# Local attention in one kernel: units of four heads by 128 keys, stacked blocks of 64 queries, and a rotary sum moved to GpSimd

## The reference

```
h = shift_token(x); q, k, v = split(h @ wqkv)
q, k = rotary_xpos(l2norm(q) * qs, l2norm(k) * ksc)
sim = (8 q) k^T over the keys of a query's own block of 64 and of the block before
      masked where key > query or key < query - 64
x = x + softmax(sim) v @ wo
x = x + feed_forward(layer_norm(shift_token(x)))
```

## Time and profile before

| what | value |
|---|---|
| time before, median of 3 runs | 2269.81 us (2269.67 to 2273.56) |
| the profiled execution, its own time | 2267.61 us |
| its span in the profile | 2265.8 us |
| mean granted TensorE clock over the span | 0.938 |
| busy over the span: PE, DVE, ACT, POOL | 1887.1, 1730.5, 1326.7, 840.5 us |

### The profile page before, as it was taken

One profiled execution on the slowest core, in us unless ns is written; L12 is line 12 of the kernel. 1 busy time (PEld: TensorE's weight loads), 2 busy tenths in 40 slices (PEclk: granted clock), 3 DMA queues, 4 the chain that ended last, 5 costly groups with the idle time before them and its releaser, 6 DMA issues. The chain is left out here.

```text
span 2265.8 us, 38842 instructions
## 1 busy us (share of the span) xinstructions
PE 1887.1 (83%) x12576; PEld 1040.6 (46%) x12576; DVE 1730.5 (76%) x4306; ACT 1326.7 (59%) x2865; POOL 840.5 (37%) x703
## 2 busy tenths in 40 slices
PE   6888888875898988769717579999999999999985
PEld 2333333332444444434315346666656566666543
DVE  6999999994677777412166679999986899999875
ACT  5777777731444444324252368888873688888731
POOL 5777777751022222224421433333321333333211
PEclk8999999995999999879958889999999999999997
DMA  5333333203011111023171400000001000000011
GB/s 152 116 100 113 109 115 117 89 29 99 23 36 43 39 37 43 23 82 109 45 210 51 132 24 6 6 1 1 2 4 26 1 6 6 1 1 1 4 35 29
DMA packets 102297, 117.06 MB, mean 52 GB/s; under 512 B 27780, under 2 KB 78255, under 8 KB 101104
## 3 DMA queue, kind: packets, MB, share of 16 engines
q1 hardware_dynamic: 98000, 106.51, 16.1%
q0 software_dynamic: 4096, 8.06, 1.1%
HBM read 71.44 MB, written 38.11 MB: 48 GB/s over the span
## 5 line engine op out<-in xcount | busy, mean ns | idle before, releaser
L392 POOL TENSOR_TENSOR m_bu<-m_dtu,m_brow 128x1024 f32<-128x1024 f32 x128 | 300.4, 2360 | 58.8 <-DVE m_hs L807 57.0
L807 DVE TENSOR_TENSOR_SCAN m_hs<-m_ps_da,m_bu 128x1024 f32<-128x1024 f32 x128 | 291.9, 2281 | 3.6 <-POOL m_bu L392 2.5
L1355 ACT ACTIVATE a_pt<-a_ps_s 128x1024 f32<-128x1024 f32 x128 | 131.1, 1025 | 227.5 <-PE a_ps_s L1133 227.5
L2851 ACT ACTIVATE l_pe<-l_ps_s,l_nbias,l_qs 128x192 f32<-128x192 f32 (+1 forms) x512 | 244.8, 487 | 32.3 <-DVE l_nbias L3007 32.3
L513 PE MATMUL m_ps_y_ps<-m_prod,m_ident 128*128 128x512 f32 x512 | 248.4, 608 | 0.0
L1472 DVE TENSOR_REDUCE a_mpad<-a_ps_s 128x4 f32<-128x1024 f32 x128 | 156.8, 1225 | 93.7 <-PE a_ps_s L1125 92.7
L1125 PE MATMUL a_ps_s<-a_heads 32*128 32x256 f32 x1024 | 187.9, 447 | 44.3 <-DVE a_mpad L1472 28.5
L659 ACT ACTIVATE m_ps_da<-m_dt,m_a_neg 128x510 f32<-128x510 f32 x256 | 166.0, 681 | 72.2 <-DVE m_hs L807 71.9
L1133 PE MATMUL a_ps_s<-a_qm,a_heads 32*128 32x256 f32 x1024 | 184.7, 437 | 1.8 <-ACT a_pt L1355 1.4
L2623 PE MATMUL l_ps_s<-l_kT,l_qT 128*128 128x384 f32 (+1 forms) x512 | 179.9, 433 | 0.0
L2861 ACT COPY l_pT<-l_ps_t 128x256 f32<-128x256 f32 (+1 forms) x256 | 122.9, 480 | 72.5 <-PE l_ps_t L2633 45.8
(11 more groups left out here) (336 smaller groups left out, 4454.6 us busy)
## 6 DMA issues: line engine op xcount, KB each, us to landing
m_brow<-state_rows SPq DMA_DIRECT2D x64, 512.0 KB, 4.3
slots<-m_void SPq DMA_DIRECT2D x16, 516.0 KB, 5.4
e_xs<-slots SPq DMA_DIRECT2D x16, 258.0 KB, 2.7
ys<-m_void SPq DMA_DIRECT2D x8, 512.0 KB, 5.4
qk<-a_qk SPq DMA_DIRECT2D x16, 256.0 KB, 2.0
a_heads<-qk SPq DMA_DIRECT2D x64, 64.0 KB
ew_w<-in_w SPq DMA_DIRECT2D x2, 2048.0 KB, 11.6
e_yy<-ys SPq DMA_DIRECT2D x16, 256.0 KB, 5.4
```

Source lines behind the costliest of these rows:

```text
L392: nc.gpsimd.tensor_tensor(bu[s % 4][:, :, :], dtu[p][:, :, :], b2, ALU.mult).then_inc(bu_rd, 1)
L807: dve.tensor_tensor_scan(hs[s % 4][:, :, :].rearrange("p h t -> p (h t)"), da[s % 2][:, :, :, :].rearrange("p h q t -> p (h q t)"), bu[s % ...
L2851: nc.scalar.activation(pe_[u % 2][:, h, 0:nk], s_ps[u % 2][:, h * 192:h * 192 + nk], ACT.Exp, bias=nbias[:, u % 2, h:h + 1], scale=qs[b % ...
```

## The change

It rewrites the attention of both local layers and leaves the feed-forward as it is.

- A unit is now four heads by 128 keys (`HU = 4`, `NU = 2` units a chunk, `U = 4` units a sequence). `maxima`, `exps`, `divide`, `transpose_p` and `p_copy` work on 4 x 128 columns in both chunks. `divide` is one product with a broadcast operand in place of one scaling per head.
- In chunk 1 each block of 64 queries has its own window of 128 keys, and the two blocks are stacked on partitions 0 to 63 and 64 to 127 of the same bank: four matmuls with 64 stationary columns in place of one with 128. `weigh` in chunk 1 takes 64 columns at a time, eight matmuls a unit, all with fresh accumulation.
- The first block's values lie across the two chunks. `bring_near` on SP copies them into a buffer `near` in the right order of partitions, by two DMAs from SBUF to SBUF a sequence, and PE waits for them ahead of chunk 1's first `weigh`. SP issues it ahead of `gather` in its queue.
- The queries' `rotary_sum` goes from DVE to POOL (the keys' stays on DVE).
- `hT` is doubled, `v` has three buffers in place of four, the waits follow.
- All three `attend` functions are written out anew, with another order, shown below for PE and DVE.

```
     def scores(n, b, u):
...
+        at_least(pe, l.ex_rd, HU * (i - 1))
+        bank = s_ps[u % 2][:, :].rearrange("p (h k) -> p h k", h=HU)
+        pe.matmul(bank, identb[:, :], mask[:, c, :, :], start=True, stop=False, ...)
+        for k in range(2):
+            j = 2 * d + k
+            if c == 0:
+                last = pe.matmul(bank[:, 2*k:2*k+2, :], qT[p][:, j, 0:P], kT[p][:, :, j, 0:P], ...)
+            else:
+                for r in range(2):
+                    q0 = P + r * HD
+                    last = pe.matmul(bank[r*HD:(r+1)*HD, 2*k:2*k+2, :], qT[p][:, j, q0:q0+HD],
+                                     kT[p][:, :, j, q0-HD:q0+HD], ...)
+        last.then_inc(l.s_mm, 1)
...
     def weigh(n, b, u):
+        else:      # chunk 1: for k, r, h
+            vals = near[(NB * n + b) % 2][:, :] if r == 0 else v[z][:, 1, :]
+            last = pe.matmul(dst, vals[:, cols], pT[u % 2][:, 2*k+h, r*HD:(r+1)*HD], start=True, ...)
...
     def divide(n, b, u):
+        dve.wait_ge(l.ex_rd, HU * (i + 1))
+        dve.reciprocal(ri[:, :], rs[:, u % 2, :]).then_inc(l.ri_s, 1)
+        dve.tensor_tensor(pn[u % 2][:, :, :], pe_[u % 2][:, :, :],
+                          ri[:, :].unsqueeze(2).to_broadcast([P, HU, P]), ALU.mult).then_inc(l.pn_rd, 1)
...
     def bring_near(n, b):                                        # SP
+        sp.wait_ge(l.v_sb, NCH * (b + 1))
+        sp.dma_start(near[k % 2][0:HD, :], v[z][HD:P, 0, :]).then_inc(near_in, 16)
+        sp.dma_start(near[k % 2][HD:P, :], v[z][0:HD, 1, :]).then_inc(near_in, 16)
...
     def rotary_sum(l, b, c):                                     # POOL, queries
+        pool.wait_ge(l.rot_rd[Q], i + 1)
+        nc.gpsimd.tensor_tensor(c1[Q][:, :, :], c1[Q][:, :, :], c2[Q][:, :, :], ALU.add)...
```

More of the change, by code:

```diff
@@ new lines, in attend @@
+                    scores(n, b, 0)
+                    if not first:
+                        transpose_p(n, b - 1, U - 1)
+                    if last < 2:
+                        project(n, b + 1, 0, Q)
+                    if not first:
+                        weigh(n, b - 1, U - 2)
+                        if last < 2:
+                            pe.wait_ge(l.v_sb, NCH * (b + 1))
+                        else:
+                            pe.wait_ge(l.res_rd, NCH * (b - 1))
+                        output(n, b - 1, 0)
@@ new lines, in attend @@
+                    scores(n, b, 1)
+                    transpose_p(n, b, 0)
+                    turn_k(n, b, 1)
+                    if not first:
+                        weigh(n, b - 1, U - 1)
+                    if last < 2:
+                        turn_q(n, b + 1, 0)
+                        if not first:
+                            pe.wait_ge(l.res_rd, NCH * (b - 1) + 1)
+                        project_v(n, b + 1, 0)
+                        project(n, b + 1, 0, K)
+                    scores(n, b, 2)
@@ new lines, in attend @@
+                    if not first:
+                        square_sums(n, b, 1, K)
+                        divide(n, b - 1, U - 1)
+                    if last < 2:
+                        rotary(n, b + 1, 0, Q)
+                    if not first:
+                        residual(n, b - 1, 0)
+                    scale_k(n, b, 1)
+                    maxima(n, b, 1)
+                    if last < 2:
+                        square_sums(n, b + 1, 0, Q)
+                    divide(n, b, 0)
+                    if last < 2:
+                        rotary(n, b + 1, 0, K)
+                        rotary_sum(n, b + 1, 0, K)
@@ new lines, in attend @@
+                    maxima(n, b, 2)
+                    if last < 2:
+                        square_sums(n, b + 1, 0, K)
+                    divide(n, b, 1)
+                    if last < 2:
+                        rotary(n, b + 1, 1, Q)
+                    if not first:
+                        residual(n, b - 1, 1)
+                    if last < 2:
+                        scale_k(n, b + 1, 0)
+                    else:
+                        norm_stats(n, 0)
+                    maxima(n, b, 3)
@@ L3050, in norm_stats @@
+                    if last < 2:
+                        square_sums(n, b + 1, 1, Q)
+                    divide(n, b, 2)
+                    if last < 2:
+                        rotary(n, b + 1, 1, K)
+                        rotary_sum(n, b + 1, 1, K)
                 def norm_stats(n, g):
```

332 lines of the change are left out of this document (157 added, 175 removed).

## The result

| | kernel before | kernel after |
|---|---|---|
| median of 4 runs | 2269.74 us (2269.61 to 2273.56) | 2647.24 us (2643.44 to 2666.53) |
| ratio, 95% interval | | 1.1672 [1.1627, 1.1717] |
| span of the profiled execution | 2265.8 us | 2648.0 us |
| mean granted clock over the span | 0.938 | 0.887 |

The change makes the kernel 377 us slower, by the medians. The forecast was 2622 us, range 2485 to 2745. Of the 382 us between the two spans, 366 lie in the two attention stages, from the first scores to the first feed-forward matmul: 374.2 us became 561.8, and 375.1 became 553.1. The rest lies at the layers' starts, between the first `transpose_r` and the first stage (4.7 us) and between the two stages (6.4 us), and 5.7 us in stretches that the change doesn't touch.

The account below looks back on a forecast made before the run. PE was taken as the bound, busy 22.86 of 23.56 us a sequence. Work 20.2 plus waits 11.3 gave 31.5, with clock falls 35.0; (35.0 - 23.56) x 31 = 355 us on 2267.6 gave 2622 us, range 2485 to 2745.

Parts of the forecast that it names:

- the sign: In the profile, `transpose_p` would wait for DVE's probabilities 2.5 to 3.3 us in every unit, 128 times.
- The round trip: PE idles from scores until DVE's maxima, `square_sums` and `divide` end: 2.51 us a unit, all waits 11.3 a sequence.
- the extra in the keys' two steps: In two steps DVE does the keys' rotary and sum before the maxima, lengthening PE's wait by 0.77 and 0.47 us.
- PE's own work: Transposes, scores and weighing in the new units: PE's work falls from 22.86 to 20.2 us a sequence.
- the 2.3 end: Chunk 1 scores per unit if changing tiling mode drains the array without overlap: 2.3 us, 1.8 a sequence more.
- The 0.3 in the sum for entering and leaving the form: Chunk 1 scores: about 0.3 us a unit for switching into and out of half-width matmuls, within the 1.40 taken.
- Period at full clock: One attention sequence without clock falls: 20.2 work plus 11.3 waits, 31.5 us against 23.56.
- About two falls in four waits: PE's clock drops after some attention waits, each fall costing 1.63 us; the sequence is taken as 35.0 us.
- The clock stays up: Rival: attention waits never lower PE's clock; 2513 us, or 2495 with half-width forms at their low ends; chance 0.18.
- The second rival: Half-width matmuls run one after the other and the clock falls after every wait: 2784 us, milder 2700 to 2750; chance 0.12.
- What the rest costs: nothing.: In attention, DVE's, ACT's and POOL's changed work and the DMAs of `near` stay covered; POOL's added sum is 1.2 us.
- a rival with 0.05: Attention waits are hidden and PE's smaller work counts: period 20.2 us, 2164 us if transposes never waited; chance 0.05.

Follow-up runs that it names:

- e2: Changed kernel with DVE's `square_sums` moved from between `maxima` and `divide` to behind `divide`; 1.1015 of the kernel before.
- r2: Changed kernel reordered: PE's `transpose_p` at the end of the next step, ACT's `exps` ahead of `p_copy`, DVE's `residual` ahead of a `rotary`; 0.9881 of the kernel before.
- r3: The kernel of r2 with the queries' rotary sum back on DVE; 0.9708 of the kernel before.
- e3: Changed kernel with nine useless bf16 matmuls of 512 columns on PE ahead of each wait for `divide`; 1.1123 of the kernel before.
- e4: Changed kernel with the queries' rotary sum back on DVE, order otherwise kept; 1.1542 of the kernel before.
- r4: Kernel before with only the queries' `rotary_sum` moved from DVE to POOL; 1.0162 of the kernel before.
- e1: Changed kernel with DVE's `divide` of the previous unit moved ahead of `maxima`, PE's order kept; 1.0447 of the kernel before.
- s3: The kernel of r3 without `bring_near` and PE's wait for it, first block weighed with wrong values; 0.969 of the kernel before.

## Why the prediction was right, and where it was off

- **The mechanism** is the forecast's: the transposes wait for `divide` in every unit. e2 shows the wait following DVE's queue, and r2 shows it and the whole loss gone with another order of the same instructions. PE waited 126 times, 2.41 to 3.32 us in the sequence shown, where 128 times 2.5 to 3.3 were named as the sign.
- **The round trip.** Forecast 11.3 us a sequence, measured 11.3 (3.17 + 2.42 + 3.32 + 2.41); the round trip itself is 2.42 where 2.51 was summed, and the extra in the keys' two steps is larger than forecast: 0.91 for 0.77 (chunk 0) and 0.75 for 0.47 (chunk 1). The two errors cancel, which is luck.
- **PE's own work.** Scores in chunk 1: 1.40 taken, 1.45 measured; weighing in chunk 1 0.75 and 0.61; chunk 0 1.10 and 1.08, 0.59 and 0.59; four transposes 0.53 and 0.44. In r3 a sequence less its four waits for DVE (0.21 + 0.68 + 0.27 + 0.44) is 19.7 us, forecast 20.2. The half-width passes do overlap: the 1.45 less 0.22 for the mask is 1.23, where eight passes of 0.22 one after the other would be 1.76. So the 2.3 end, for which the prediction called on the Trainium skill, didn't come. The 0.3 in the sum for entering and leaving the form had no row behind it; 1.23 less the summed 0.88 leaves 0.35.
- **Period at full clock.** Forecast 31.5; e3, 31.56 at clock 1.00. That it fits to 0.1 us is partly luck: PE's own work is 0.5 us less than summed, while `scale_k` beside POOL's sum puts one of the waits up by 0.38, and PE waits another 0.38 ahead of `transpose_r` for a residual; the sum had both at nothing.
- **The clock.** "About two falls in four waits" and 35.0 us; the sequence shown has two slow stretches and 34.31 us, and the mean over both layers is 23.56 + 366/31 = 35.4. "The clock stays up" is what e3 makes by force (1.1123). The second rival failed on both of its conditions: the scores of chunk 1 take 1.45 and not 2.3, and the clock doesn't fall after every wait. How often a wait lets the clock fall isn't explained: in that sequence it was after the two waits of over 3 us, in e2 a fall follows one of 1.81 us and none follows 2.71.
- **The stages.** Forecast +355 us, measured +366. The span rose by 27 us more than forecast: 11 in the stages, whose clock differed a little between the two (0.85, 0.87) and which I didn't follow further, 11 at the layer starts, a term that I left out because I counted the steady state alone (PE waits 15.7 us there for POOL's sum, in three places), and 6 in parts that the change doesn't touch.
- **"What the rest costs: nothing."** This is the step that failed in kind, though its size here is small. Its cover is the round trip: with `divide` late anyway, DVE can lose time (e4: 26 to 28 us, 10 of them at the starts). DVE's own work was 17.4 us a sequence where about 16 was summed, which cost nothing here either. I looked only at whether POOL's sum would be ready in time, and priced it as 1.2 us on an engine with room (measured 1.29). I didn't ask what it does to DVE. Where DVE is close to PE's pace the sum on POOL costs 30 us in the stages (r2 against r3) and 26 in the kernel before (r4), and 9 and 12 us more at the layers' starts, where PE waits for it. The Trainium skill (SBUF — State Buffer, SBUF: two separate sides) says that DVE and GpSimd share a pair of SBUF ports under an exclusive lock: a DVE instruction with two SBUF inputs and a GpSimd instruction that reads SBUF block one another for the whole instruction, whichever starts first. By that rule the sum should have been a rival of its own; the trace agrees with it for the sum, in e1 (0.68 to 1.74) and in r4 with both orders of arrival. It doesn't for POOL's powers, which also read SBUF and under which DVE's scaling kept its 0.16 us in r4; so "the whole instruction" doesn't hold for each of them, and there the measurement decides. The DMAs of `near` were rightly priced at nothing (s3: 1 us a stage at most).
- **What could still be gained.** The forecast's smaller PE work was real: in r3 PE is busy 19.45 us a sequence in place of 22.86, and the period is 21.32 in place of 23.56. The forecast took it as a rival with 0.05, rightly for this order.

## What to carry to other kernels

In a software pipeline written out by hand, look at each pair of engines for who stands between a result and its use: if a step's consumer follows its producer at once on one queue and the maker of its input stands behind the same producer on another, the engine stops for the whole chain, whatever the sizes. Here one step of distance was worth 400 us, far more than the smaller instructions. Moving an elementwise operation with SBUF operands from DVE to POOL isn't free for DVE even if both have room; look for DVE instructions with two SBUF operands that start during it. And a wait that covers something else (here ACT's copy of a shared bank) is only worth removing if the cover stays.

## What the runs showed that I had not expected

- POOL's addition of 512 columns and DVE's instructions with two SBUF operands held one another up in the rows shown, and in r4 in all 60 places. The price is up to nearly the whole of the other instruction: a 0.68 us product took 1.74, a scaling of two columns 0.79 in place of 0.16, and POOL's sum 1.66 in place of 1.27 when it came second. A maximum out of PSUM that ran during the sum in r4 kept its 0.55 us. POOL's powers of 8 columns didn't hold up DVE's scaling in r4, but in the changed kernel they take 1.93 us in place of 1.67 in the 120 places where the product of `divide` has started ahead of them.
- Extra matmuls can make a kernel faster: nine bf16 matmuls in each wait, of no use to the result, gave back 115 us by keeping the clock at 1.00. PE's way from the scores to the transposes became longer in one step of four only.
- Sixteen passes of 64 columns with 64 stationary columns took 0.61 us, eight of 128 columns 0.59. So at these sizes halving the length and doubling the count cost next to nothing.
